# Adapter rows gathered once, and a new order of the first stages

## The reference

```
x1 = x + x @ w0[lora_id[b]].T                       # one 512x512 weight a sequence
a  = x1[b] @ a_n[attn_id[b]]        n = q, k, v     # rank 16 adapters
q  = rope(x1 @ wq + aq @ bq[attn_id[b]])            # 32 heads of 128
k  = rope(x1 @ wk + ak @ bk[attn_id[b]])            # 8 heads of 128
v  = x1 @ wv + av @ bv[attn_id[b]]                  # 8 heads of 128
x2 = x1 + (softmax(causal(q k^T / sqrt(128))) v) @ wo + adapter
x3 = x2 + rank 16 product;   out = x3 + x3 @ W.T + b + 2 * rank 16 product
```

## Time and profile before

| | us |
|---|---|
| median of 3 timed runs | 825.22 (823.1, 825.22, 829.45) |
| the profiled execution | 820.86 |
| its span | 819.2 |
| PE busy in it | 752.1 (92%) |
| DVE, ACT, POOL busy | 543.8, 324.1, 325.6 |
| moved by DMA | 87.87 MB |

### The profile page before, as it was taken

The page is one execution under the profiler, slowest core; times in us unless marked ns, Lnnn a source line. Parts: engine busy times, 40 slices in busy tenths (PEclk is TensorE's granted clock), DMA queues, the critical chain, the costliest instruction groups (busy, mean ns, idle before and its releaser), DMA issues. The chain is left out here.

```text
span 819.2 us, 13219 instructions
## 1 busy us (share of the span) xinstructions
PE 752.1 (92%) x4100; PEld 625.0 (76%) x4100; DVE 543.8 (66%) x1362; ACT 324.1 (40%) x902; POOL 325.6 (40%) x280
## 2 busy tenths in 40 slices
PE   2888897985889999999999999999999999998798
PEld 2777785764668888888888888888888888876586
DVE  3645577676576767767677667758676875654983
ACT  3555343011153454354345435336343533542540
POOL 2334351453374273346237236335523723510320
PEclk8798997997899999999999999999999999999899
DMA  8776787264313024013212303301311110720502
GB/s 265 232 282 201 223 259 226 96 220 167 128 65 117 1 74 164 9 64 118 61 45 83 115 0 121 123 0 64 132 47 55 73 38 3 161 20 7 128 25 78
DMA packets 61498, 87.87 MB, mean 107 GB/s; under 512 B 18118, under 2 KB 35686, under 8 KB 57878
## 3 DMA queue, kind: packets, MB, share of 16 engines
q1 hardware_dynamic: 41714, 73.53, 27.8%
q10 hardware_dynamic: 17188, 8.46, 3.5%
q0 software_dynamic: 2560, 5.45, 2.2%
HBM read 72.45 MB, written 19.68 MB: 112 GB/s over the span
## 5 line engine op out<-in xcount | busy, mean ns | idle before, releaser
L980 POOL TENSOR_TENSOR prob<-prob,rinv 128x512 f32<-128x512 f32 x64 | 66.6, 1041 | 215.6 <-DVE rinv L1064 215.6
L919 ACT ACTIVATE ot_hi<-ps_p_o 128x512 fp32r<-128x512 f32 x64 | 38.0, 594 | 214.7 <-PE ps_p_o L1128 214.7
L78 PE MATMUL ps_p_q<-x1t_hi,wgt_hi 128*128 128x512 f32 x280 | 115.9, 414 | 0.8 <-DVE qt L618 0.8
L973 POOL TENSOR_TENSOR qt<-qc,qs 128x512 f32<-128x512 f32 x60 | 83.7, 1395 | 77.8 <-DVE qs L1008 77.8
L929 ACT ACTIVATE prob<-sm,nmax 128x128 f32<-128x128 f32 x256 | 99.8, 392 | 31.2 <-DVE nmax L1049 30.1
L80 PE MATMUL ps_p_q<-x1t_hi,wgt_lo 128*128 128x512 f32 x280 | 110.9, 396 | 0.0
L79 PE MATMUL ps_p_q<-x1t_lo,wgt_hi 128*128 128x512 f32 x280 | 110.8, 396 | 0.0
L1140 PE MATMUL ps_p_out<-wo_hi,ot_hi 128*128 128x512 f32 x256 | 101.9, 398 | 6.6 <-DVE ot_lo L1026 4.7
L1141 PE MATMUL ps_p_out<-wo_lo,ot_hi 128*128 128x512 f32 x256 | 101.4, 396 | 0.0
L1142 PE MATMUL ps_p_out<-wo_hi,ot_lo 128*128 128x512 f32 x256 | 100.8, 394 | 0.0
L1008 DVE TENSOR_TENSOR qs<-ps_p_q,trig 64x512 f32<-64x512 f32 x120 | 82.6, 688 | 3.7
(11 more groups left out here) (227 smaller groups left out, 1693.8 us busy)
## 6 DMA issues: line engine op xcount, KB each, us to landing
raw_w<-in_wq SPq DMA_DIRECT2D x8, 1024.0 KB, 4.9
raw_b<-bq_sel SPq DMA_DIRECT2D x64, 128.0 KB
wo_raw<-in_wo SPq DMA_DIRECT2D x8, 1024.0 KB, 4.9
qt<-in_w SPq DMA_DIRECT2D x5, 1024.0 KB, 9.1
v_hi_d<-v_hi ACTq DMA_DIRECT2D x16, 256.0 KB, 3.7
v_lo_d<-v_lo ACTq DMA_DIRECT2D x16, 256.0 KB, 5.3
kt<-k_rot SPq DMA_DIRECT2D x16, 256.0 KB, 3.7
v_hi<-v_hi_d SPq DMA_DIRECT2D x16, 256.0 KB, 3.9
```

The lines of the kernel that those rows point to most:

```text
L78: pe.matmul(bank[:, :], w_hi[:, k, cols], x1t_hi[:, k, tok], start=(k == 0), stop=False)
L973: pool.tensor_tensor(qt[:, half, h, :], qc[:, :], qs[:, :], ALU.add).then_inc(q_done, 1)
L980: pool.tensor_tensor(prob[i][:, :, :], prob[i][:, :, :], rinv[i][:, :].unsqueeze(2).broadcast_to([P, G, T]), ALU.mult).then_inc(prob_done, 1)
```

## The change

- `bk` and `bv` come as one array `bkv`. POOL gathers the rows of each sequence to `bkv_sel` in HBM: block 0 before stage 0 (8 DMAs of 32 KB), blocks 1 to 3 in stages 1 to 4 (8 DMAs of 96 KB). SP then loads a pack by one DMA with a fixed address, four copies x 32 rows, so 4 a block and none with an id to read. The pack has its low parts in the upper 64 partitions; DVE cuts 64 partitions by a `tensor_tensor` where it made a `scalar_tensor_tensor` of 128 with the table `lows`, which is gone. The same holds in the attention groups.
- SP loads `x`, the adapters and `w0` of sequences 0 to 2 ahead of wv 0; wv 1 follows `w0` of sequence 4; block 1's rows come after all of the first product's loads.
- On PE, `product(s)` is first in its stage, and the parts of `adapters`, `turn_x1` and `turn_ax` stand between the matmuls of the products and values. On ACT and DVE the cut of `w0(s+1)` and the addition stand ahead of the adapters' and x1's cuts; the cut of value unit n moves from stage n+2 to n+3.
- `PIECES` changes; block 4's weights come before block 3's, and their low parts go to POOL. The first queries are units 28 to 31, with the last four key units behind them.
- `gather_bq` loses its second DMA (`ao`, now in stages 20 to 27); `gather_last` moves to the first group of the attention. The first loads of `wo` wait for all 36 units.

Added lines and some of their surroundings; the lines that they replace stand in the kernel above.

```diff
+W_ORDER = (0, 1, 2, 4, 3)
+
+UNIT_OF = [(blk, u) for blk in range(3) for u in range(UNITS)]
+UNIT_OF += [(3, u) for u in range(G)] + [(4, u) for u in range(G)] + [(3, u) for u in range(G, UNITS)]
+KEYS = [n for n, (blk, u) in enumerate(UNIT_OF) if blk in (2, 3)]
...
+PIECES = {1: [(0, "w", k) for k in range(KC)] + [(0, "b", 0)], 2: [(0, "b", 1)], 3: [(0, "b", 2)], 4: [(0, "b", 3)],
+          6: [(1, "b", 0)], 7: [(1, "w", 0), (1, "w", 1), (1, "b", 1)], 8: [(1, "w", 2), (1, "w", 3), (1, "b", 2)], 9: [(1, "b", 3)],
+          10: [(2, "w", 0)], 11: [(2, "w", 1), (2, "b", 0)], 12: [(2, "w", 2), (2, "b", 1)], 13: [(2, "w", 3), (2, "b", 2)],
+          14: [(2, "b", 3)], 15: [(4, "w", 0)], 16: [(4, "w", 1)], 17: [(4, "w", 2)], 18: [(4, "w", 3), (3, "b", 0)],
+          19: [(3, "b", 1)], 20: [(3, "w", 0), (3, "b", 2)], 21: [(3, "w", 1), (3, "b", 3)], 22: [(3, "w", 2)], 23: [(3, "w", 3)]}
...
+    PIECES[26 + k] = [(4, "b", k)]
...
-
-    src = (bv, bv, bk, bk)[j]
-    cols = slice(j % 2 * GW, (j % 2 + 1) * GW)
-    for b in range(2 * pairs[0], 2 * pairs[-1] + 2):
-        pick = dma.value_load(id_rows[0:1, 1, b:b + 1], min_val=0, max_val=src.shape[0] - 1)
-        four_times(dma, b, src[bass.DynSlice(pick, 1), :, cols], raw_b_in[b // 2])
...
+    for p in pairs:
+        rows = bkv_sel[j] if j < 4 else bq_sel[0]
+        four_times(dma, p, rows[2 * p:2 * p + 2].rearrange("(a two) r n -> a (two r) n", a=1), raw_b_in[p])
+
+def four_times(dma, p, rows, done):
+
+    dma.dma_start(raw_b[:, p, :], rows.broadcast_to([4, 2 * R, GW])).then_inc(done, 16)
...
+        def load_v0_rows(p):
+            sp.wait_ge(v0_gathered[p // 2], 16 * HALF)
+            load_block_b(sp, 0, [p])
...
+        for b in range(2):
+            load_x(b)
+            load_a(b)
+        load_w0(2)
         load_block_w(sp, 0)
...
+        load_v0_rows(0)
         load_x(2)
         load_a(2)
+        load_v0_rows(1)
         for b in range(RAW, B):
...
+                load_v0_rows(2)
+                load_v0_rows(3)
+            if b == 4:
+                sp.wait_ge(*low_parts(0, KC))
                 load_block_w(sp, 1)
...
+        sp.wait_ge(b_lo_done, PAIRS)
+        sp.wait_ge(vk_gathered, 16 * B)
+        load_block_b(sp, 1, range(PAIRS))
+        sp.wait_ge(*low_parts(1, KC))
+        load_block_w(sp, 2)
         sp.wait_ge(b_lo_done, 2 * PAIRS)
+        load_block_b(sp, 2, range(PAIRS))
+        sp.wait_ge(*low_parts(2, KC))
+        load_block_w(sp, 4)
+        sp.wait_ge(b_lo_done, 3 * PAIRS)
+        load_block_b(sp, 3, range(PAIRS))
+        sp.wait_ge(*low_parts(4, KC))
         load_block_w(sp, 3)
...
+        for m, n in enumerate(KEYS):
...
-            sp.wait_ge(k_done, m + 1)
+            sp.wait_ge(k_done, n - VU + 1)
             sp.dma_start(k_rot[g, :, h * HT:(h + 1) * HT], kr[h]).then_inc(k_out[h], 16)
...
+            if m == 3:
                 for i in range(VR):
                     sp.wait_ge(v_out[i], 32 * len(range(i, VU, VR)))
                 for i in range(2):
                     sp.wait_ge(k_out[i], 16)
                 load_kv(sp, 0, 0)
                 load_kv(sp, 0, 1)
+            if m == 4:
                 sp.wait_ge(b_lo_done, 4 * PAIRS)
+                sp.wait_ge(bq_gathered, 16 * B)
+                load_block_b(sp, 4, range(PAIRS))
+            if m == 6:
+                sp.wait_ge(*low_parts(3, KC))
+                load_wq(sp, 1)
...
+                sp.wait_ge(b_lo_done, 5 * PAIRS)
+                load_bq(sp, 1, 0)
+                load_bq(sp, 1, 1)
+        sp.wait_ge(p_ready, KU + G)
+        sp.wait_ge(gathered, 16 * B)
         load_wo(sp, 0)
...
+            if 1 <= n <= VU:
+                store_v(n - 1)
             if 0 <= n < VU:
                 act.wait_ge(p_ready, n + 1)
                 if n >= VR:
                     act.wait_ge(v_out[n % VR], 32 * (n // VR))
                 act.activation(v_hi[n % VR][:, :], ps_p[n % 4][:, :], ACT.Copy).then_inc(v_hi_done, 1)
             if s + 1 < B:
+                split_xt(s + 1)
+                split_w0(s + 1, 0, KC // 2)
+            if s < B:
+                split_a(s)
+            if s + 1 < B:
                 split_w0(s + 1, KC // 2, KC)
+            if 1 <= s <= B:
+                pack_hi(s - 1)
+            if s > 1:
+                split_pieces(s)
+            if s < B:
+                split_x1(s)
+            if 1 <= s < B:
+                copy_axt(s - 1)
+            if s == B + 1:
+                copy_axt(B - 1)
+            if s == 1:
                 split_pieces(s)
             if s == 11:
+                act.wait_ge(tab, 8)
                 act.activation(sin_t, sin_t, ACT.Sin).then_inc(sines, 1)
...
+                    low = packs[PACK[j]][P // 2:P, k, :]
                     dve.wait_ge(b_hi_done, PAIRS * j + k + 1)
+                    dve.tensor_tensor(low, raw_b[P // 2:P, k, :], low.bitcast(F32), ALU.subtract).then_inc(b_lo_done, 1)
...
+            n = s - 3
             if 0 <= n < VU:
                 dve.wait_ge(v_hi_done, n + 1)
                 dve.tensor_tensor(v_lo[n % VR][:, :], ps_p[n % 4][:, :], v_hi[n % VR][:, :].bitcast(F32), ALU.subtract).then_inc(v_lo_done, 1)
+            if 2 <= s < B - 1:
+                split_w0(s + 1, 0, KC // 2)
             if s < B:
                 add(s)
+            if 1 <= s <= B:
+                pack_lo(s - 1)
+            if s < 2:
+                split_w0(s + 1, 0, KC // 2)
+            if s + 1 < B:
+                split_w0(s + 1, KC // 2, KC - 1)
+            if s < B:
+                split_x1(s)
+            low_pieces(s)
             tables(s)
+            n = s - 2
...
+        def gather_v0(b):
+            a = pool.value_load(id_rows[0:1, 1, b:b + 1], min_val=0, max_val=bkv.shape[0] - 1)
+            pool.dma_start(bkv_sel[0, b].rearrange("(a r) n -> a r n", a=1), bkv[bass.DynSlice(a, 1), 0]).then_inc(v0_gathered[b // HALF], 16)
...
+        def gather_vk(b):
+            a = pool.value_load(id_rows[0:1, 1, b:b + 1], min_val=0, max_val=bkv.shape[0] - 1)
+            pool.dma_start(bkv_sel[1:4, b], bkv[bass.DynSlice(a, 1), 1:4].rearrange("a j r n -> (a j) r n")).then_inc(vk_gathered, 16)
...
+        pool.wait_ge(ids_in, 32)
+        for b in range(HALF):
+            gather_v0(b)
         split_xt(0)
+        for b in range(HALF, B):
+            gather_v0(b)
         for s in range(LAST):
             n = s - 2
             if s + 1 < B:
                 split_xt(s + 1)
+            if s < B:
+                split_a(s)
+            if s + 1 < B:
                 split_w0_end(s + 1)
+            if 1 <= s <= HALF:
+                gather_vk(2 * s - 2)
+                gather_vk(2 * s - 1)
...
+            for j, kind, k in PIECES.get(s, []):
+                if kind == "w" and j in (2, 4):
+                    pool.wait_ge(w_hi_done, KC * W_ORDER.index(j) + k + 1)
+                    pool.tensor_tensor(wgt_lo[WGT[j]][:, k, :], raw_w[:, k, :], wgt_hi[WGT[j]][:, k, :].bitcast(F32),
+                                       ALU.subtract).then_inc(w_lo_pool, 1)
             if 8 <= s < 8 + B:
                 gather_bq(s - 8)
...
+            if 20 <= s < 20 + B:
+                gather_ao(s - 20)
...
+                if blk < 4:
+                    at = KEYS.index(n)
+                    if at >= 2:
+                        pool.wait_ge(k_out[at % 2], 16 * (at // 2))
+                    rotated = kr[at % 2]
+                else:
+                    rotated = qt[:, 0, u, :]
...
+                for at, (x_part, w_part) in enumerate(((xt_hi, hi), (xt_hi, lo), (xt_lo, hi))):
+                    mm = pe.matmul(ps_y[i][:, :], x_part[i][:, row], w_part[:, k, :], start=(k == at == 0), stop=(k == KC - 1 and at == 2))
+                    if k == KC - 1 and at == 2:
+                        mm.then_inc(y_ready, 1)
+                    if b and k:
+                        adapter_part(b - 1, 3 * (k - 1) + at)
...
+            if m == 0:
+                pe.wait_ge(x1t_lo_done, b + 1)
+                pe.wait_ge(a_lo_done, b + 1)
+                if b >= 1:
+                    pe.wait_ge(axt_done, b)
+            x_part, a_part = ((x1t_hi, a_hi), (x1t_hi, a_lo), (x1t_lo, a_hi))[m % 3]
+            mm = pe.matmul(ps_a, x_part[:, k, cols], a_part[i][:, k, :, :], start=(m == 0), stop=(m == 3 * KC - 1))
+            if m == 3 * KC - 1:
+                mm.then_inc(ax_ready, 1)
...
+            for i in range(3 * KC):
+                k = i // 3
+                if b == 0 and i % 3 == 0:
+                    pe.wait_ge(*low_parts(blk, k + 1))
+                x_part, w_part = ((x1t_hi, hi), (x1t_hi, lo), (x1t_lo, hi))[i % 3]
+                pe.matmul(o, x_part[:, k, tok], w_part[:, k, :], start=(i == 0), stop=False)
+                if s < B and i < 3:
+                    adapter_part(s - 1, 9 + i)
+                if s < B and i == 4:
+                    turn_x1(s)
+                if s < B and i >= 9:
+                    turn_ax(s - 1, i - 9)
+                if s == B:
```

(33 more changed lines are left out.)

220 lines of the change are left out of this document (52 added, 168 removed), and 4 rows, old and new, of the table PIECES.

## The result

After the change the kernel takes 830.42 us, median of 20 runs (828.37 to 831.38), against 824.11 (820.75 to 829.45) before: a ratio of 1.0069, 95% interval 1.0056 to 1.0083. The forecast was 792, with 773 to 808 as its range. The profiled execution spans 829.1 us, 9.9 more than before.

The account below looks back on a forecast made before the run. PE bounds the kernel, with waits and slow clock to win only before 213 us: 44.8 - 3 - 4 - 5 - 2 + 0.7 = 31.5 us gained, giving 793.7, stated as 792 us; range 773 to 808.

Parts of the forecast that it names:

- What bounds the kernel: PE is full from 250 to 700 us; up to 213 us, 45.5 us of waits and 19.3 of slow clock can be won.
- Prices: At full clock a long matmul costs 0.233 us, an adapter matmul 0.11; work up to 213.1 us is 148.2 us.
- the other end, 0.02: Lowest price in us of an adapter part between two long matmuls; it would gain 8.4 us over the 0.11 taken.
- The opening: Stages 0 and 1: first product 0.7 us later, second from about 16.8 us, stage 2 starting at 26.3 us.
- Loads in stages 3 to 7: 3 us: A stage's 2.65 MB in 7.9 us needs 335 GB/s, just inside 377; 3 us set against the gain.
- a rival with 0.17: Value stages: other engines bound them, the four DMA engines with rows needing 108 to 125 us; 804 us, chance 0.17.
- the slower rival: Stages 2 to 7: w0 too late in each, PE at half clock, 42 us lost in six stages; 833 us, chance 0.05.
- In orders that follow the data: Stages 2 to 7: ACT, DVE and POOL have 4 to 6 us of work a stage, ordered so PE sets the pace.
- From values to keys: DVE lags, late value stores hold ACT, unit 16 waits for a low part: 3 us and 1 of slow clock.
- Unit 29: Block 4's pack is whole at about 149.5 us, wanted at 147: 2.5 us of wait and as much slow clock.
- The attention: Two gathers in slot 1 cost 2 us; the query's 3.6 us wait goes, first probabilities wait about 2.9, net 0.7 won.
- PE should set the pace: Stages 2 to 7 at 7.9 us each, bound by PE; wrong if PE idles above 35 us up to the last unit.

Follow-up runs that it names:

- e14: e9 with the attention's first keys and values loaded after key store 10, not 4, and query group 1's weights after 11, not 6: 793.67 us, ratio 0.9622.
- e1: The changed kernel with a stage's twelve adapter parts in one run behind the product, not one after each long matmul: 830.72 us, ratio 1.0071.
- e8: The changed kernel with one plain row load per copy, all pairs in it, plus adapter parts in one run behind the product: 802.3 us, ratio 0.974.
- e3_bq: The changed kernel with query group 1's row loads behind the last key store and the load of wo, as before the change: 831.88 us, ratio 1.0081.
- e4_spread: The changed kernel with each fourfold row load as four plain loads of 32 partitions, same bytes: 797.65 us, ratio 0.9671.
- e7: The changed kernel with one plain row load per copy, plus POOL's first low part of xt ahead of its eight gathers: 804.06 us, ratio 0.9753.
- e11: The changed kernel with plain row loads for blocks 1 to 4 and the query groups, block 0 keeping the fourfold source: 804.77 us, ratio 0.9761.
- e9: e4_spread with block 4's rows asked for after key store 3, ahead of the attention's first keys and values: 797.87 us, ratio 0.9687.
- e12: e9 with the key stores issued on ACT's queue in place of SP's, except the last: 798.05 us, ratio 0.9686.

## Why the prediction was wrong, by its own steps

In one sentence: the prediction let a fourfold row load occupy its four engines for itself, 2.7 us each, and gave nothing for what other loads and stores lose that need the same four; with the loads spread and nothing else changed, 33 of the 41 us by which it missed the profile are gone. The terms in turn:

**What bounds the kernel: right.** The middle did not move, and the gain was to be had in the first 213 us; e14's 793.67 shows that it is there, at nearly the 792 forecast, but in another kernel.

**Prices: right.** Stages 4 to 7 are 7.9 apart to 0.05. The adapter part, whose price between long matmuls was unknown, costs the 0.11 that was taken. PE's timeline of the changed kernel at full clock:

```profile
67.39 0.48 PE L727 MATMUL ps_y_s<-wgt_lo,v_hi 128*128 128x512 f32 x1
67.71 0.18 PE L753 MATMUL ps_ax_ao<-a_lo,x1t_hi 128*128 128x48 f32 x1
67.73 0.47 PE L727 MATMUL ps_y_s<-wgt_hi,v_lo 128*128 128x512 f32 x1
```

A pair takes 0.34 us = 0.233 + 0.11; the other end, 0.02, is out, as e1 and e8 say as well, so nothing of the 8.4 us was there to gain. At half clock the pair takes 0.64 (22.15 to 22.79), so a short one 0.21 there, not the 0.11 that the opening's sum used.

**The opening: right in the main.** The third product starts at 28.1 in the profile of the changed kernel, at half clock, and at 26.2 in e3_bq and 26.35 in e4_spread, 26.3 forecast. POOL's gathers are 1.11 apart, not 0.83, so the first product starts 2.1 us late, not 0.7; the second still waits 1.0 for w0(1), and e7, which starts early again, gains nothing.

**"Loads in stages 3 to 7: 3 us": the failed step, first part.** It divided the bytes of a stage by the traffic of all sixteen engines, 335 GB/s of 377. But the rows stand on four engines only (share 0.25), w0's loads land after 16.2 us at the median where plain rows leave 12.2, and the stage waits for w0. The stages were 11 us later than this term allowed, 14 in all. With plain loads the same stage 7's turn comes at 76.81 against 76.5 forecast: the term was about right for spread loads and wrong for these. The 0.3 is luck: in the other kernels with block 0's loads plain it comes between 74.4 and 78.4, in e7 at 81.4. The prediction had all the pieces: the earlier trace rows for the four engines, and the sum of 108 to 125 us for them, but as a rival with 0.17, and in the forecast only as a duration of the rows themselves (2.7 us), never as a delay of what stands behind them.

The mechanism of the slower rival, w0 too late in each stage, is what happened in stages 2 and 3, at 0.05. Its price was wrong both ways: two stages were hit, not six, and the slow clock, which it made 5 us a stage, was worth nothing (e1). It had no share in the later 25 us.

One part of these stages stays untested. DVE cuts the first half of w0(s+1) ahead of the addition of stage s, so that a late w0 stops the turn and the value unit as well. In the changed kernel that cut of w0(3) is done at 38.4 and `product(3)` starts at 44.03; with the addition first, PE could do in its wait what now stands between the two, some 5 us a stage by these two numbers (an estimate). "In orders that follow the data" passed over this. No run moves the addition.

**"From values to keys" 4 and "Unit 29" 5: the failed step, second and larger part.** From stage 7's turn to the last unit's end the changed kernel takes 128.5 us, the prediction's terms give 103.8. The trace shows 8.4 us of waits on low parts, 11.1 on the pack and 2.5 on the keys' rotation. These two windows, of the changed kernel and of e4_spread:

```profile
87.50:216.00 128.50, 105.48 (x443) 83.38 (x442) 85.92 (x113) 29.58 (x50) 46.17 (x41) 0.92 0.55 183
```
```profile
76.80:188.20 111.40, 99.88 (x443) 80.19 (x442) 85.51 (x113) 29.37 (x50) 47.57 (x42) 0.97 0.67 211
```

Without its 9 us of waits the forecast's work is 94.8. The changed kernel is 33.7 over that, 22 of them waits and most of the rest slow clock; e4_spread is 16.6 over, with 11.0 of waits (7.4 for the pack, 2.5 for the rotation, 1.1 for low parts). That the cause is the rows' shape is shown by e11, which takes 20 us out of this stretch. "The key store behind it waits as today" did hold: POOL waits 25.1 us for stores in all, 25.4 before. Mis-sized were two waits. The stores of the values were in the term ("Values stored late hold ACT"), but as relieved; they land after 10.5 us, 5.0 with plain rows, and the waits on low parts are 8.4 us where the term had 3. The pack's are 11.1 where it had 2.5. A part of what holds the pack in e4 and e9 is a full DMA system, which the prediction did not look at there: it moved rows, keys, weights and gathers into one place. e14 shows that for half of it; the other 4 us are open.

**The attention.** The turn of probabilities waits 6.9, not 2.9; with plain loads it is 2.6. The two gathers in the slots were given 2 us: from the fourth scores (246.50) to the fourth from last (729.61) the changed kernel takes 483.1 us, the kernel before 480.7 (239.21 to 719.90), so 2.4. No wait on `qt` stands before the first scores, as forecast.

**"PE should set the pace": wrong by its own test.** PE was to be idle for 35 us at most up to the last unit; up to 216 us it is idle for 216 - 173.2 = 42.8. In e4_spread, up to 188.2 us, for 28.4.

**The page's rule.** The prediction set the Trainium skill ("DMA: Bandwidth & Descriptors", section "Rules for kernel authors"), by which a leading broadcast of c copies keeps a load on at most c engines, against the part of the four loads, and drew from it only that the transfer gains nothing. The runs agree with the rule at 0.25 of the engines and 89 GB/s, and the loads that fall under it cost 33 us here.

## What to carry to other kernels

When rows of a profile show a low DMA share beside a busy queue, ask which other loads and stores have pieces on the busy engines; the mean traffic does not tell (238 GB/s over the first 100 us here, 239 before the change, while w0's median landing went from 9.1 us to 16.2, and was 12.2 with plain rows). Look at the source's outermost dimension before the order of the work is rebuilt. And half clock in a stretch in front of a wait may cost nothing, as in e1: take it off and see whether the wait grows by as much.

## What the runs showed of the hardware that was not expected

- Two row loads with a fourfold source hold SP's issue for 8.01 us at 22 us, between w0(3) and w0(4); eight plain ones of the same bytes take 3.66 at the same place.
- The same opening runs in two ways. From 20 to 40 us the changed kernel's profile has PE busy for 18.8 us at a granted clock of 0.51 and 0.50, that of e3 for 11.8 us at 0.89 and 0.80; the turns come at 39.1 and 54.4, and at 39.2 and 54.3 us.
- A 256 KB key store, 2.0 us at its quickest, took 10.0 us on ACT's queue at a DMA share of 0.9 to 1.05 (e12), and 11.8 behind four fourfold row loads on SP's, at a mean share of 0.34 (changed kernel, 213 to 225 us).
